# Narrow-column variance and row-banded spreading in the second normalisation, with the sort steps cut in halves between them

## The reference, cut to what matters

```python
x = x + _L0_conv_ref(_ln_c(x), L0_conv_weight, L0_conv_bias)
t = _to_tokens(x)
t = t + _L0_ffn_ref(_ln_t(t), L0_ffn_W_gat, ..., L0_ffn_edge_index)
...
def _ln_t(v, eps=1e-05):
    m = jnp.mean(v, axis=-1, keepdims=True)
    s = jnp.var(v, axis=-1, keepdims=True)
    return (v - m) / jnp.sqrt(s + eps)
```

## Time and profile before

| | us |
|---|---|
| median of 3 runs | 4735.66 |
| lowest and highest | 4731.93, 4740.96 |
| time of the profiled execution | 4737.77 |
| its span in the trace | 4736.0 |
| TensorE busy | 3866.3 (82%) |
| GpSimd busy | 2844.5 (60%) |
| VectorE busy | 2657.0 (56%) |
| ScalarE busy | 942.1 (20%) |

### The profile page before, as it was taken

How to read it: one execution, slowest core, us unless ns; L and a number is a source line. 1 busy time by engine, 2 the same in 40 slices (tenths; PEclk the granted TensorE clock), 3 DMA queues, 4 the chain that set the end, 5 groups by cost and what they waited for, 6 DMA issues and landing times. The chain is left out here.

```text
span 4736.0 us, 62817 instructions
## 1 busy us (share of the span) xinstructions
PE 3866.3 (82%) x21121; PEld 2690.0 (57%) x21121; DVE 2657.0 (56%) x3261; ACT 942.1 (20%) x2069; POOL 2844.5 (60%) x2881
## 2 busy tenths in 40 slices
PE   4785333799948999999999999999999999661499
PEld 1453223577736666666666666666666667561122
DVE  7779999667644444444444444444444444447666
ACT  0110000000012333332333333333333333110000
POOL 2001888766626777777777777777777777771000
PEclk8897555788867888988888988889888888776699
DMA  1232111788862111111111111111111111682498
GB/s 48 69 96 74 49 47 35 85 107 102 102 107 49 34 35 34 36 35 35 35 35 35 35 35 35 35 33 37 32 38 33 35 35 34 10 10 3 137 289 247
DMA packets 323403, 284.04 MB, mean 60 GB/s; under 512 B 201074, under 2 KB 279154, under 8 KB 322804
## 3 DMA queue, kind: packets, MB, share of 16 engines
q1 hardware_dynamic: 213732, 200.98, 19.9%
q0 software_dynamic: 91008, 30.58, 11.5%
q10 hardware_dynamic: 18576, 51.39, 2.8%
HBM read 160.41 MB, written 122.31 MB: 60 GB/s over the span
## 5 line engine op out<-in xcount | busy, mean ns | idle before, releaser
L1074 POOL DMA_INDIRECT gath<-tab_d,src_no x2288 | 2158.9, 944 | 775.8 <-issue 696.9
L446 POOL DMA_INDIRECT edge_d<-run_slots,slots x544 | 657.2, 1208 | 662.8 <-ACT run_slots L636 502.2
L1204 PEld LDWEIGHTS C<-spread,lo_hot 128*128 128x128 f32 x4576 | 848.1, 244 | 331.3 <-DVE spread L1359 173.7
L1204 PE MATMUL C<-spread,lo_hot 128*128 128x160 f32 x4576 | 920.2, 370 | 139.4 <-DVE spread L1359 139.1
L1193 PEld LDWEIGHTS C<-dst_rows,lo_hot_t 128*128 128x128 f32 x4576 | 586.7, 208 | 91.1 <-issue 78.3
L1371 DVE TENSOR_TENSOR acc<-acc,C 128x160 f32 x572 | 183.5, 321 | 796.3 <-PE C L1204 746.8
L1193 PE MATMUL C<-dst_rows,lo_hot_t 128*128 128x32 f32 x4576 | 603.9, 289 | 11.2 <-ACT lo_hot_t L1092 11.2
L1214 PE MATMUL A<-T,w1s 64*128 64x392 f32 x1024 | 533.8, 605 | 0.0
L1097 ACT ACTIVATE hid<-A,b1s 128x392 f32<-128x392 f32 x512 | 300.6, 587 | 1078.9 <-PE A L1214 1078.9
L557 PE MATMUL C<-wide_rec,hot_lo 128*128 128x136 f16 x2048 | 266.8, 305 | 296.9 <-DVE wide_rec L814 296.9
L1225 PE MATMUL A<-hid,w2s 128*64 128x392 f32 x1024 | 456.3, 528 | 0.0
(11 more groups left out here) (263 smaller groups left out, 3195.6 us busy)
## 6 DMA issues: line engine op xcount, KB each, us to landing
mlp_d<-mlp ACTq DMA_DIRECT2D x128, 392.0 KB
mlp<-mlp_d SPq DMA_DIRECT2D x64, 784.0 KB, 4.7
gath<-tab_d,src_no POOLq DMA_INDIRECT x2288
pixels<-in_x SPq DMA_DIRECT2D x32, 392.0 KB, 8.1
src<-in_x SPq DMA_DIRECT2D x32, 392.0 KB, 9.2
T<-t_d SPq DMA_DIRECT2D x128, 98.0 KB
X<-x_d SPq DMA_DIRECT2D x64, 196.0 KB, 5.4
out<-X SPq DMA_DIRECT2D x128, 98.0 KB, 2.6
```

The costliest lines, as they stand in the source:

```text
L446: pool.indirect_dma_start(edge_d, bass.IndirectOffsetOnAxis(ap=slots[:, k, c:c + 1], axis=0), run_slots[:, k, c * RUN:(c + 1) * RUN, :].re ...
L1074: pool.indirect_dma_start(gath[:, g % BUFS, j, :], None, tab_d, bass.IndirectOffsetOnAxis(ap=src_no[:, t:t + 1], axis=0)).then_inc(gathere ...
L1204: mm = pe.matmul(C[:, bank, at:at + HI * VALS], lo_hot[:, k, u * U + j, :], spread[:, u * U + j].rearrange("p h v -> p (h v)"), start=(j = ...
```

## The change

Four things change, all in the image stage but for the constants.

- **Variance.** The 14 matmuls of step 6 become 4. S is now the moving operand, 392 columns at a time, and the stationary operand is the new constant `thin`, 128 x 32, with 1/64 in column h for the partitions of half h and zeros elsewhere. Chunk c goes to output partitions 32c to 32c + 31 of bank 0 of A, that is, to its own quarter of TensorE's columns. The variances so lie as 128 x 392, with two useful partitions in each quarter.
- **Root, reciprocal, spreading.** ScalarE and VectorE work on the 128 x 392 tile `std2`. The 28 matmuls of step 8 become 4: chunk c takes the 32 partitions of its quarter, of `std2` and of the new constant `fan` (a 1 where row c * 32 + h meets the columns of half h), and writes bank c of A. The final multiply is one instruction over all four chunks.
- **Order on TensorE.** Each sort step is cut in halves of 16 matmuls. The four halves stand behind the mean, the variance, the spreading and the convolution. `project` of image b stands at the end of image b, behind the convolution of image b + 1, and no longer between mean and variance of the next image; ScalarE's `rows_out` moves with it.
- **Order on VectorE.** `hot_lo` of j = 1 is written before the subtraction, `hot_col` and `spread_step` of j = 1 behind it, ahead of the reciprocal. `group_places` moves from there to behind the final multiply.

On TensorE, for the second image of a pair (here images 0 and 1, the rows without loop instructions), before: mean, projection, variance, a whole sort step, spreading, convolution of the next image, a whole sort step.

The diff, without the parts of `one_hot_step` and `sort_step` that only add the argument for halves:

```diff
+                link(pool, pool.memset(thin[:], 0.0), step)
+                for h in range(2):
+                    link(pool, pool.memset(thin[h * CH:(h + 1) * CH, h:h + 1], 1.0 / CH), step)
+                link(pool, pool.memset(fan[:], 0.0), step)
+                for c in range(CHUNKS):
+                    for h in range(2):
+                        link(pool, pool.affine_select(out=fan[:, h * CH:(h + 1) * CH], ..., base=-(c * QUAD + h), ...), step)
...
                         pe.wait_ge(s["summed"], b + 1)
                         mean_of(pe, X[k], s["mean2_ready"])
-                        if not (isinstance(b, int) and b == 0):
-                            project(b - 1, 1 - k)
+                        if sorts:
+                            sort_step(g, 1 - k, 0, 0)
                         pe.wait_ge(s["squared2"], b + 1)
-                        variance_of(pe, k, s["var2_ready"])
-                        if not (last and k == 1):
-                            sort_step(g, 1 - k, 0)
+                        for c in range(CHUNKS):
+                            mm = pe.matmul(A[c * QUAD:(c + 1) * QUAD, 0, 0:CHUNK], thin[:], S[:, c, :], start=True, stop=True)
+                        mm.then_inc(s["var2_ready"], 1)
+                        if sorts:
+                            sort_step(g, 1 - k, 0, 1)
                         pe.wait_ge(s["rstd2_ready"], b + 1)
-                        spread_rstd(pe, A, s["rstd2_spread"])
+                        for c in range(CHUNKS):
+                            mm = pe.matmul(A[:, c, 0:CHUNK], fan[c * QUAD:(c + 1) * QUAD, :], std2[c * QUAD:(c + 1) * QUAD, :], start=True, stop=True)
+                        mm.then_inc(s["rstd2_spread"], 1)
+                        if sorts:
+                            sort_step(g, 1 - k, 1, 0)
                         pe.wait_ge(s["tokens_ready"], b + 1)
-                        if not (last and k == 1):
+                        if sorts:
                             convolve(i + k, 1 - k)
-                            sort_step(g, 1 - k, 1)
+                            sort_step(g, 1 - k, 1, 1)
+                        project(b, k)
...
                         act.activation(S[:], D[k], ACT.Square).then_inc(s["squared2"], 1)
-                        if not (isinstance(b, int) and b == 0):
-                            rows_out(b - 1)
                         act.wait_ge(s["var2_ready"], b + 1)
-                        deviations(eps_t, k, s["deviated2"])
+                        act.activation(std2[:], A[:, 0, 0:CHUNK], ACT.Sqrt, bias=eps_t[:]).then_inc(s["deviated2"], 1)
                         if not (last and k == 1):
                             group_out(i + SG // 4 + k, 1 - k)
+                        rows_out(b)
...
                             spread_step(*at, 0)
+                            dve.wait_ge(s["spread_steps"], (at[0] * 2 + at[1]) * 2 * FIELDS + FIELDS)
+                            one_hot_step(*at, 1, 0)
                         dve.wait_ge(s["mean2_ready"], b + 1)
...
                         dve.tensor_tensor(D[k], X[k], A[:, :, 0:CHUNK], ALU.subtract).then_inc(s["centred2"], 1)
                         if sorts:
+                            one_hot_step(*at, 1, 1)
+                            spread_step(*at, 1)
+                        dve.wait_ge(s["deviated2"], b + 1)
+                        dve.reciprocal(std2[:], std2[:]).then_inc(s["rstd2_ready"], 1)
+                        dve.wait_ge(s["rstd2_spread"], b + 1)
+                        dve.tensor_tensor(D[k], D[k], A[:, :, 0:CHUNK], ALU.mult).then_inc(s["tokens_ready"], 1)
+                        if sorts:
                             group_places(*at)
-                        dve.wait_ge(s["deviated2"], b + 1)
-                        dve.reciprocal(rstd[:], dev[:]).then_inc(s["rstd2_ready"], 1)
-                        if sorts:
-                            one_hot_step(*at, 1)
-                            spread_step(*at, 1)
-                        dve.wait_ge(s["rstd2_spread"], b + 1)
-                        scale(D[k], A, s["tokens_ready"])
```

More of the change, by code:

```diff
@@ L43 @@
 assert QCHUNKS * QGROUPS == GROUPS_P
+QUAD = P // CHUNKS
 MAGIC = 1.5 * 2.0 ** 23
@@ L186, in build @@
         fold = sb("fold", [P, CH])
+        thin = sb("thin", [P, QUAD])
+        fan = sb("fan", [P, P])
         A = ctx.enter_context(nc.psum_tensor("A", [P, 4, 512], F32))
@@ L208, in build @@
             Q = [tb(f"Q{k}", [P, HALF_ROWS + 2, WID + 2], BF16) for k in range(2)]
+            std2 = tb("std2", [P, CHUNK])
             dev = tb("dev", [TOK, TOK_TILES, 2])
@@ L417, in _ @@
                     link(pool, pool.memset(halves[h * CH:(h + 1) * CH, h * CH:(h + 1) * CH], 1.0 / CH), step)
+                link(pool, pool.memset(thin[:], 0.0), step)
[4 more added lines that the diff above has]
+                    for h in range(2):
+                        link(pool, pool.affine_select(out=fan[:, h * CH:(h + 1) * CH], in_=fan[:, h * CH:(h + 1) * CH], compare_op=ALU.not_equal, fill=1.0,
+                                                      base=-(c * QUAD + h), pattern=[[0, CH]], channel_multiplier=1), step)
                 link(pool, pool.memset(eps_c[:], 1e-6), step)
@@ L548, in _, with sort_step @@
                 pe.wait_ge(s["w_ready"], 1)
-                def sort_step(g, k, j):
-                    if j == 0 and not (isinstance(g, int) and g < 2):
-                        pe.wait_ge(s["group_out"], g - 1)
-                    pe.wait_ge(s["spread_steps"], (g * 2 + j + 1) * FIELDS)
+                def sort_step(g, k, j, part=None):
+                    if part != 1:
+                        if j == 0 and not (isinstance(g, int) and g < 2):
+                            pe.wait_ge(s["group_out"], g - 1)
+                        pe.wait_ge(s["spread_steps"], (g * 2 + j + 1) * FIELDS)
                     fields = wide_rec[:, j].rearrange("p n v c t -> p n (v c) t")
-                    for t in range(STEP):
+                    for t in range(STEP) if part is None else range(part * STEP // 2, (part + 1) * STEP // 2):
                         mm = pe.matmul(C[:, k, 0:FIELDS * SLOT_COLS], hot_lo[:, j, t // LINE, :, t % LINE], fields[:, t // LINE, :, t % LINE],
                                        start=(j == 0 and t == 0), stop=(j == 1 and t == STEP - 1))
-                    mm.then_inc(s["step_sums"], 1)
+                    if part != 0:
+                        mm.then_inc(s["step_sums"], 1)
                 pe.wait_ge(s["base_ready"], 1)
@@ L622, in _ @@
                 image_pair(B // 2 - 1, True)
-                project(B - 1, 1)
             @block.scalar
@@ L684, in _ @@
                 image_pair(B // 2 - 1, True)
-                rows_out(B - 1)
             @block.vector
@@ L794, in take, with one_hot_step @@
                                         C[:, h * 2:h * 2 + 2, :].rearrange("p k n -> p (k n)")).then_inc(s["ranks_taken"], 1)
-                def one_hot_step(i, k, j):
+                def one_hot_step(i, k, j, which=None):
                     g = i * 2 + k
-                    if not (isinstance(g, int) and g == 0):
+                    if which != 1 and not (isinstance(g, int) and g == 0):
                         dve.wait_ge(s["step_sums"], g * 2 + j - 1)
@@ L807, in lanes @@
                         return lane_h[:, 0:n, :].rearrange("p (k c) t -> p k c t", k=1).broadcast_to([P, LINES, n, LINE])
-                    L(dve.tensor_tensor(hot_lo[:, j], lanes(P), over(slot_lo[:, cols], P), ALU.is_equal))
-                    L(dve.tensor_tensor(hot_col, lanes(SLOT_COLS), over(slot_col[:, cols], SLOT_COLS), ALU.is_equal))
+                    if which != 1:
+                        L(dve.tensor_tensor(hot_lo[:, j], lanes(P), over(slot_lo[:, cols], P), ALU.is_equal))
+                    if which != 0:
+                        L(dve.tensor_tensor(hot_col, lanes(SLOT_COLS), over(slot_col[:, cols], SLOT_COLS), ALU.is_equal))
                 def spread_step(i, k, j):
@@ L957, in image_pair @@
                         if sorts:
-                            group_places(*at)
-                        dve.wait_ge(s["deviated2"], b + 1)
-                        dve.reciprocal(rstd[:], dev[:]).then_inc(s["rstd2_ready"], 1)
-                        if sorts:
-                            one_hot_step(*at, 1)
-                            spread_step(*at, 1)
-                        dve.wait_ge(s["rstd2_spread"], b + 1)
-                        scale(D[k], A, s["tokens_ready"])
+                            one_hot_step(*at, 1, 1)
[5 more added lines that the diff above has]
+                        if sorts:
+                            group_places(*at)
                 image_pair(0)
-                with rolled(dve, 1, B // 2 - 1, step, 2 * (1 + SORT_LINKS)) as i:
+                with rolled(dve, 1, B // 2 - 1, step, 2 * SORT_LINKS) as i:
                     image_pair(i)
```

6 lines of the change are left out of this document (1 added, 5 removed).

## The result

The changed kernel takes 4676.36 us (median of 4 runs, 4672.4 to 4679.9), the kernel before 4738.31 us (4 runs, 4731.93 to 4742.18): a ratio of 0.987, 95% interval 0.9853 to 0.9887. That is 62 us less; the forecast's sum had 68 us less, and its time was 4670 us. The profiled execution took 4679.9 us. The change acts where it was expected to; some sizes were off, above all the wait for the spreading.

A forecast was written before the change was run, and what follows sets the result against it. TensorE's own work was taken to bound an image. At 26.4 us per image, 4.3 less, the last subtraction moves to 1267.8 and the next block to 1290.4 or 1291; gain 68, forecast 4670 us, range 4655 to 4712.

The forecast's parts named there:

- Column groups and row bands: TensorE's narrow matmuls: four quarters run together, variance 0.85 us for 2.91, spreading by row bands 1.0 us.
- serial bands: Rival on the spreading: row bands run one after another, 2.81 us, 28.2 an image, 4697 us; chance 0.13.
- both serial: Rival on TensorE: variance and spreading both run serially, 29.2 us an image, 4712 us; chance 0.06.
- Per image 26.4: Image stage: VectorE's and TensorE's rounds nearly equal and disturbing one another, 26.4 us per image, 4.3 less than before.
- the sum by busy time: VectorE's round from its busy time: 21.24 - 0.33 - 1.94 + 2.61 + 1.79 = 23.4, plus 1.1 + 1.1, gives 25.6 us.
- The two worked rounds: Image stage: VectorE's round 25.6 to 26.2 us, TensorE's 25.5, or 26.1 with a convolution partly at the low clock.
- the variance's cover: Squares, variance and root end 4.9 us after the mean, VectorE is free at 5.8: variance hidden by up to 0.9 us.
- The sum: Image stage's end: last subtraction from 1332.1 to 1267.8, next block at 1290.4, 1291 by GpSimd; gain 68 us.
- Set-up: Before the image stage: 13 more GpSimd constants of about 0.3 us, costing nothing; 4 us without their cover.
- The rival of the GpSimd bound: Image stage: GpSimd's scatters take 27.4 us a group, 1.0 more an image, 4685 us; chance 0.07.
- DMA: Rival in the image stage: loads for image b + 2 come some 1 us late each time, 4685 us; chance 0.04.
- The clock: Slower rival: TensorE, waiting more, stays at 1.2 GHz; its round becomes 38.4 us, the kernel 4853 us; chance 0.05.

The follow-up runs named there:

- e3: The changed kernel with the spreading on the whole array, four matmuls of 128 rows one after another; 6505.94 us, ratio 0.9712 to the kernel before, on chip A.
- e4: The changed kernel with the variance on the whole array, four accumulating matmuls of 128 stationary columns; 6536.17 us, ratio 0.9768 to the kernel before, on chip A.
- g2: The changed kernel with 48 of the sort group's 64 products per image left out; 4690.24 us, ratio 0.9888 to the kernel before, on chip B.
- g1: The changed kernel with each of the convolution's 36 products per image cut into two of half the columns; 4677.53 us, ratio 0.9864 to the kernel before.
- f3_fill: The changed kernel with the first operation of group_places between reciprocal and wait for the spreading; 6519.53 us, ratio 0.9633 to the kernel before, on chip A.

## Why the prediction was right, point by point

*What bounds before, and that it goes away.* Right: variance and spreading were 5.8 of TensorE's 28 busy us per image, and with the narrow forms in their place and the new order the image fell by 4.0 us.

*Column groups and row bands.* Forecast 0.85 and 1.0 us, measured 0.87 to 1.54 and 0.94 to 1.69, by the clock. The rivals of serial bands and of both serial fall with that, and e3 and e4 show what serial would have been (2.90). The prediction said that the trace agrees weakly with a drain at a change of mode; its own row, a step without a gap, spoke against one that can be seen.

*Reciprocal, root, multiply* as the rows had them: 2.60, 0.59, 1.79. VectorE's busy time per image was to be 23.4 and is 23.43.

*Per image 26.4; measured 26.69.* The term that was mis-sized is the wait for the spreading, 1.1 us with its hand-over in the sum by busy time. It is 1.81 in twelve of 13 images, 1.75 on average, since the spreading comes after TensorE has waited for squares and reciprocal and mostly finds the lower clock. That is 0.65 us per image. The rest of VectorE's round is 23.43 busy, 0.27 of waits for the convolution before the sum and 1.30 of joints (the small gaps between instructions) and small waits: 26.75. (The prediction's sum by busy time adds 1.1 twice and explains only the first.) The two worked rounds were 25.6 to 26.2 and 26.1; 26.4 was set above both by judgement, and that took up part of what was missing, so the closeness of the number is in part luck. TensorE's round lost what the forecast had in hand as well: the variance's cover was to be up to 0.9 us and is 0.03 and 0.54 in the two images read.

*The sum.* First subtraction 870.4 for 871.8, last 1270.7 for 1267.8, its multiply's end 11.1 us later for 11.7, from there 11.3 to the next block for 10.9: 1293.1 for 1290.4. That is 2.7 of the 6.4 us by which the median lies over the forecast. The remaining 3.7 are of the size by which executions differ. The kernel before came out at 4738.31 us, where the forecast started from 4735.66. And the last stage, from the first gated product to the end, took 290.4 us in this profile and 280.5 in that of before, with the same program. (Taken strictly the prediction's sum gives 4670.8 for an execution like the profiled one, and with its 2 us off 4668.8; it was rounded to 4670.)

*Set-up.* Forecast 4 us of constants, hidden. The eight selects that fill `fan` took 8.48 us, not 0.3 each, so GpSimd's last constant ends 6.6 us later than before; it is hidden all the same (the first subtraction came 1.4 us earlier).

*GpSimd.* Forecast gap under 2 us and "almost the bound". Both hold: its longest wait between groups is 1.5 us in the 13 images, and it works 26.5 us a group for an image of 26.75. But nothing waits for it, so it does not set the pace. The rival of the GpSimd bound falls, by a narrow margin.

*DMA.* No wait for a load stands before the convolution, at a share of 0.99. The rival falls.

*The clock.* The one rival on the slow side did not come: 0.82, and the convolution takes 6.22 to 7.48 us, 6.6 on average, where it was 6.22 in two images of three and 7.88 in the third. But its mechanism exists in small. It is the 0.65 us above, and g2 shows it with more idle time: 0.75, and a slower image from less work.

*TensorE's new waits* were 30.1 and 18.1 us in 13 images, 2.3 and 1.4 each; forecast 1.3 to 2. The first is longer than forecast since in eleven of the 13 images VectorE subtracts later than the mean is ready, which the forecast's TensorE round had at nothing.

## What to carry to other kernels

A reduction or a spreading that uses a quarter of the array's rows or columns can be run four abreast in a third of the time, but count what it moves to the element-wise engine: here a reciprocal eight times as dear became part of the bound, and in the variant with few products 2.2 us less of it were worth 2.0 us per image, down to the pace that GpSimd sets. A short product that comes right after a wait should be priced at the lower clock (1.69 us for 0.94 in twelve of 13 images), and taking work off a TensorE that doesn't bound can slow down the chain that does (g2). Read the gain on more than one chip where one can: the edit was worth 1.3% in the result and 2.7% on chip A.

## What the runs showed that was not expected

Chip A took 6697 to 6770 us (medians) for a kernel that takes 4738 elsewhere. Up to the image stage little is lost (first subtraction at 874.6 us there for 871.8). Both kernels lose nearly the same behind the image stage (from the next block's first instruction to the end 5191.0 us for the one, 5192.9 for the other, by span; 3376.7 and 3385.0 in the traces of the result), and in the image stage TensorE stands idle at issue for 94 us in 13 images of the kernel before. The stops begin after a run of products without a gap, and then come at about one every 0.7 us. Whether it is the supply of instructions or something else on that chip is open: the rate per product was not constant, and the run that was to settle it (g1) fell on chip B. Why f3_fill gained 1.9 us per image there, and what it would bring elsewhere, is open too.
